# Feeding the projections of a graph layer from an ordered copy of y, made by ScalarE one slot ahead

## What is computed

```python
def _L1_gnn_ref(H, W_lin, W_val, a, W_out, A0, src, dst):
    Xq = (H @ W_lin.T).reshape(bt, n, h, dh)
    Xv = (H @ W_val.T).reshape(bt, n, h, dh)
    e = einsum('behd,hd->beh', leaky_relu(Xq[:, src] + Xq[:, dst], 0.2), a) + log(A0[src, dst] + EPS)
    attn = softmax of e over the edges of one src
    Y = segment_sum(attn[..., None] * Xv[:, dst], src)
    return Y @ W_out.T

x = _layernorm(x + _L0_gnn_ref(x, adj, ...))
x = _layernorm(x + _L1_gnn_ref(x, ...))
```

## Time and profile before

| | us |
|---|---|
| median of three runs | 975.04 (974.39 to 976.59) |
| the profiled execution, time | 973.87 |
| its span, first to last instruction | 972.1 |
| PE busy (matmuls) | 933.5 (96%) |
| PE weight loads | 820.3 (84%) |
| DVE busy | 698.1 (72%) |
| ACT busy | 581.0 (60%) |
| POOL busy | 173.0 (18%) |

### The profile page before, as it was taken

One profiled execution on the slowest core, in us unless ns is written; L12 is line 12 of the kernel. 1 busy time (PEld: TensorE's weight loads), 2 busy tenths in 40 slices (PEclk: granted clock), 3 DMA queues, 4 the chain that ended last, 5 costly groups with the idle time before them and its releaser, 6 DMA issues.

```text
span 972.1 us, 15304 instructions
## 1 busy us (share of the span) xinstructions
PE 933.5 (96%) x5411; PEld 820.3 (84%) x5411; DVE 698.1 (72%) x1560; ACT 581.0 (60%) x1084; POOL 173.0 (18%) x509
## 2 busy tenths in 40 slices
PE   7999999989999999999999999999999999999784
PEld 6888888868777799999988877889989999988674
DVE  5777777777777877777777676675756766765874
ACT  2777777777676766767766666543434445444344
POOL 0000000000000000000000101144434443535655
PEclk9999999999999999999999999999999999999998
DMA  4212211010000000000004776735200101011112
GB/s 114 67 48 65 63 55 45 1 44 1 0 1 1 1 1 1 2 1 1 1 1 87 176 168 154 157 82 130 45 1 12 33 23 33 23 33 34 45 55 66
DMA packets 43260, 45.44 MB, mean 47 GB/s; under 512 B 2576, under 2 KB 40112, under 8 KB 40112
## 3 DMA queue, kind: packets, MB, share of 16 engines
q1 hardware_dynamic: 39504, 27.47, 9.7%
q0 software_dynamic: 2304, 16.78, 8.5%
q10 hardware_dynamic: 1376, 0.22, 0.1%
HBM read 19.29 MB, written 8.39 MB: 28 GB/s over the span
## 4 chain that ended last, share of the span: by engine, by line
PE 86%; DVE 6%; ACT 3%; issue 2%; POOL 2%; DMA 1%; ACTq 0%; DVEq 0%; POOLq 0%
PE psum L1058 12%; PE psum L443 8%; PE psum L444 8%; PE psum L445 8%; PE psum L461 6%; PE psum L457 6%; PE psum L458 6%; PE psum L1131 4%; PE psum L361 3%; PE psum L379 3%; PE psum L389 2%; PE psum L1142 2%; PE psum L352 2%; PE psum L351 2%; PE psum L353 2%
## 5 line engine op out<-in xcount | busy, mean ns | idle before, releaser
L559 ACT ACTIVATE work<-psum,bias 128x512 f32<-128x512 f32 (+1 forms) x408 | 233.7, 623 | 30.7 <-PE psum L461 30.2
L443 PE MATMUL psum<-hT_hi,w_hi 128*128 128x512 f32 (+1 forms) x408 | 148.7, 364 | 3.3 <-ACT work L559 2.6
L444 PE MATMUL psum<-hT_lo,w_hi 128*128 128x512 f32 (+1 forms) x408 | 147.2, 361 | 0.0
L445 PE MATMUL psum<-hT_hi,w_lo 128*128 128x512 f32 (+1 forms) x408 | 147.2, 361 | 0.0
L545 ACT ACTIVATE work<-work 128x512 f32<-128x512 f32 (+1 forms) x112 | 63.8, 570 | 104.5 <-DVE work L811 73.2
L1058 PE MATMUL psum<-w_qv,hT_lo 128*128 128x128 f32 x512 | 124.9, 397 | 1.0 <-DVE hT_lo L1286 1.0
L1058 PEld LDWEIGHTS psum<-w_qv,hT_lo 128*128 128x128 f32 x512 | 122.1, 328 | 1.3 <-DVE hT_lo L1286 1.2
L818 DVE TENSOR_TENSOR work<-work 128x512 f32<-128x512 f32 (+1 forms) x112 | 68.5, 612 | 54.1 <-ACT work L545 54.1
L970 POOL DMA_DIRECT2D hT_lo<-hT_hi x8 | 7.3, 918 | 556.5 <-DVE hT_lo L786 537.3
L457 PE MATMUL psum<-hs_hi,w_hi 128*128 128x512 f32 (+1 forms) x288 | 103.8, 360 | 0.8 <-DVE hs_hi L784 0.6
L461 PE MATMUL psum<-hs_lo,w_hi 128*128 128x512 f32 (+1 forms) x288 | 104.4, 363 | 0.0
(11 more groups left out here) (190 smaller groups left out, 1832.7 us busy)
## 6 DMA issues: line engine op xcount, KB each, us to landing
work<-x SPq DMA_DIRECT2D x32, 256.0 KB, 3.0
x_stage<-x_by_feature SPq DMA_DIRECT2D x8, 1024.0 KB, 5.1
hT_lo<-hT_hi POOLq DMA_DIRECT2D x8, 1024.0 KB, 8.0
hT_lo<-x_stage POOLq DMA_DIRECT2D x8, 1024.0 KB, 7.0
out<-x_kept SPq DMA_DIRECT2D x32, 256.0 KB, 2.3
work<-L_gnn_Wih SPq DMA_DIRECT2D x4, 256.0 KB, 3.2
work<-L_gnn_Whh SPq DMA_DIRECT2D x3, 256.0 KB, 3.0
bg_all<-L_gnn_bg ACTq DMA_DIRECT2D x2, 64.0 KB, 5.1
```

Of the source, the lines that this page charges most:

```text
L443: pe.matmul(out, w_hi[:, w, g, :], xh, start=True, stop=False)
L444: pe.matmul(out, w_hi[:, w, g, :], xl, start=False, stop=False)
L445: mm = pe.matmul(out, w_lo[:, w, g, :], xh, start=False, stop=(t == 0))
L559: op = act.activation(gate[s][g][:, 0:ph.width], psum[:, 4 * s + g, 0:ph.width], ACT.Tanh if g == G else ACT.Sigmoid, bias=bias[:, b:b + 1])
```

## The change

A new tensor `y_ordered` holds two tiles of y with the batch as the slow index and the node as the fast one, so that the columns of a batch are neighbours. ScalarE fills it: `order(k)` is one activation (Copy) of 128 by 512 elements that reads tile k of y four elements apart and writes it in order. It stands at the head of ScalarE's slot k - 1; `order(0)` follows `read_turned(1)` among the last LSTM steps, and `order(1)` opens slot 0. `project` waits for it and takes its stationary operand from the copy, in `queries` and in `values`. The transposes of `turn` go on reading y as before. To make room in SBUF, the ring `x1_kept` has 22 tiles in place of 24.

```diff
-    RING = LAG + 11
+    RING = LAG + 9
+    y_ordered = sb("y_ordered", [P, 2, BT, P])
-    def y_of(k, b):
-        return y_by_feature[:, k * TW:(k + 1) * TW].rearrange("p (t b) -> p b t", b=BT)[:, b, :]
+    def y_of(k):
+        return y_by_feature[:, k * TW:(k + 1) * TW].rearrange("p (t b) -> p b t", b=BT)
...
-                mm = pe.transpose(psum[:, turn_bank(k), b * P:(b + 1) * P], y_of(k, b), ident[:, :])
+                mm = pe.transpose(psum[:, turn_bank(k), b * P:(b + 1) * P], y_of(k)[:, b, :], ident[:, :])
...
         def project(k, bank, w, free, made):
+            pe.wait_ge(S["y_ordered"], k + 1)
             if k:
                 pe.wait_ge(free, k)
             for b in range(BT):
-                mm = pe.matmul(psum[:, bank, b * P:(b + 1) * P], y_of(k, b), w, start=True, stop=True)
+                mm = pe.matmul(psum[:, bank, b * P:(b + 1) * P], y_ordered[:, k % 2, b, :], w, start=True, stop=True)
...
     def enter_read(act, k):
-        read_turned, _ = scalar_steps(act)
+        read_turned, order, _ = scalar_steps(act)
         read_turned(k)
+        if k:
+            order(0)
...
+        def order(k):
+
+            act.wait_ge(S["y_made"], 16 * (k // GROUP + 1))
+            if k >= 2:
+                act.wait_ge(S["v_psum"], k - 1)
+            act.activation(y_ordered[:, k % 2], y_of(k), ACT.Copy).then_inc(S["y_ordered"], 1)
...
         def slot(n):
+            if has(n + 1):
+                order(n + 1)
             if has(n):
```

More of the change, by code:

```diff
@@ L875, in back @@
     last_pass = before.phases[-1]
-    names = ("h_summed x_staged y_made t_psum y_done stats_done q_psum v_psum q_hi xq_ready v_hi xv_ready "
+    names = ("h_summed x_staged y_made y_ordered t_psum y_done stats_done q_psum v_psum q_hi xq_ready v_hi xv_ready "
              "z_psum leaky_ready edges_psum log_added max_f max_b below_max exp_done sum_f sum_b recip_done attn_row attn_psum "
@@ L1248, in slot @@
                 leaky_relu(n, 1)
-        return read_turned, slot
+        return read_turned, order, slot
     def run_scalar(act):
-        _, slot = scalar_steps(act)
+        _, _, slot = scalar_steps(act)
         for n in range(LAST):
```

## The result

| | before | after |
|---|---|---|
| median of the runs, us | 975.18 (974.39 to 976.59) | 921.65 (919.82 to 922.66) |
| the profiled execution, time | 973.87 | 919.82 |
| its span | 972.1 | 918.0 |
| PE busy | 933.5 (96%) | 876.0 (95%) |
| PE weight loads | 820.3 (84%) | 760.3 (83%) |

The ratio is 0.9447 with a 95% interval of 0.9429 to 0.9466: 53.5 us less, where 53.0 had been forecast. The new copy is L1211.

A forecast was written before the change was run, and what follows sets the result against it. PE was taken to bound the kernel through L1058's slow loads; 33.2 + 10.6 + 7.2 + 1.3 + 1.0 - 0.3 = 53.0 us off 973.9 gives 920.9, median 922 us. Own range 913 to 933; 913 to 940 for 8 in 10.

The forecast's parts named there:

- The bound and the cause: Projections in `back`: PE bounds; operand spacing slows L1058, whose matmuls go from 233 to 112 ns, ceiling 62.1 us.
- The rival by which the change does nothing: L1058: spacing is not what slows it, pace stays 233 ns, the copy hides, 975 us; chance 0.07.
- The clock rival: Slots 2 to 12: waits bring the clock down to 1.2 GHz, about 45 us more, 967 us; chance 0.05.
- Full slots: Slots 14 to 31: 1.94 us gained in 16, 1.4 in slots 21 and 29, less 0.6 for late reciprocals: 33.2 us.
- Slots 2 to 7: Early slots: 4.14 us in place of 5.91, with a new 0.16 us PE wait on VectorE; 10.6 us gained.
- Slots 8 to 12: Slots adding softmax steps: VectorE becomes the bound, 24.3 us against 31.5; 7.2 us gained.
- Slots 0 and 1: Start of `back`: one of four halves counts, 1.0 us gained; `order(0)` loses 0.3; `order(1)` costs nothing.
- The copy: ScalarE, ahead of `query_hi` in full slots: 0.7 us, between 0.60 and 1.14, hidden since 1.25 us costs nothing.
- the first rival: Copy dearer than its cover: each us past 1.25 delays `query_hi`, VectorE, PE; at 2 us, 945 us; chance 0.10.
- the slower one: ScalarE stalls reading four apart; slower than before from 3.2 us a copy; at 3.6 us, 988 us; chance 0.05.
- POOL: Early slots: an accumulating DMA may hold it about 1 us; factors asked two slots later, 2 us to spare.
- The ring: Ring of 22: a store has four slots to reuse in place of six; no wait seen, no cost.

The follow-up runs named there:

- run 1: The changed kernel with its copy kept in y's order, so projections still read four elements apart; 974.56 us, ratio 0.9996 to the kernel before.
- run 2: The changed kernel with only `values` reading the ordered copy and `queries` reading y four apart; 948.03 us, ratio 0.9724 to the kernel before.
- Run 11: The changed kernel with the softmax reciprocals done for only 8 of every 128 columns; 920.53 us, ratio 0.9442 to the kernel before.
- run 5: The changed kernel with a cheap copy in y's order, read with neighbouring columns, so projections get other columns; 922.75 us, ratio 0.9474 to the kernel before.
- run 6: The changed kernel with `order(1)` moved to follow `order(0)` among the LSTM gates; 920.81 us, ratio 0.9446 to the kernel before.
- run 12: The kernel before with the ring of 22 tiles and an unused tensor of `y_ordered`'s size; 975.33 us, ratio 1.0006 to the kernel before.
- run 4: The changed kernel with ScalarE also copying one batch (128 elements) beside each copy of tiles 3 to 31; 921.96 us.
- run 3: The changed kernel with ScalarE making each copy of tiles 3 to 31 twice, first into a spare tensor; 925.49 us.
- run 9: On top of run 6, the last four accumulating DMAs spread over slots 1, 4, 8 and 11; 920.73 us, ratio 0.9443 to the kernel before.
- run 7: The changed kernel with `queries(0)`, `values(0)` and `queries(1)` reading y directly, without `order(0)`; 920.14 us, ratio 0.9443 to the kernel before.

## Why the prediction was right

**The bound and the cause** held. The spacing of the stationary operand slowed the loads, and the pace that I took from L1131 is the pace that came. Runs 1 and 2 show it: spacing kept, nothing; half the loads, half the gain. The rival by which the change does nothing is refuted by run 1. The clock rival didn't come either: the mean granted clock is 0.993, with falls of a few us and none through slots 2 to 12. The Trainium skill's "SBUF — State Buffer" (section "Door 1: The DMA port swizzle") can be read so that a step of four fp32 elements is free; run 1 and the changed kernel refute this for weight loads (328 against 194 ns) and for ScalarE (1.14 against 0.63 us). Its other sentence, two accesses to a line, fits both.

**Full slots** were right, and for two small terms too careful. The reciprocal slots pay nothing (7.75; `weight_values` started at 5.01 where 5.15 was reckoned), and slots 21 and 29 gained 1.6 each, not 1.4. That is 0.6 and 0.4, or 1.0 of the 1.1 us between 34.3 and 33.2.

**Slots 2 to 7** were right in size and in kind. `query_lo` ends at s + 3.02 and the first load of `gather` follows at s + 3.07, where 3.02 and 3.08 were reckoned. The slot is 4.12, not 4.14.

**Slots 8 to 12** gave 7.8 for 7.2, but the step was only in part the right one. I took VectorE's total busy time as the bound for all five slots. In fact slots 8 and 9 run at 4.12, and the loss sits in slots 10 to 12. There the chain of waits does lie on VectorE, from 681.8 to 692.2 us, but behind a load of ScalarE's table that the working didn't have. Run 11 took 1.5 us of VectorE's work away and 0.5 came back, as TensorE is close behind. So several things wait on each other in slots 10 to 12, and the near hit owes something to chance.

**Slots 0 and 1** were the step that failed: 0.7 forecast, -0.2 found. That compares one execution with one, and the start of `back` moves by more than this. The stretch from `values(1)` to slot 2 is the better measure: 4.16 us before, 4.51 after, where 1.0 less was forecast. The delay by `order(1)` is free as a wait, as I had said: `values(1)` starts at 639.96, set by VectorE (640.13 before). I left out two things. The first is the same wait of `gather` on `query_lo` that I had reckoned for slots 2 to 7; with it, runs 5 and 6 gain 0.7 of the 1.0. The second is the clock, whose fall cost the other 1.0 in the profiled execution. That the change brings this fall about is not shown. Run 5 had both pauses without it, and run 12, without any copy, had it. Over four executions each, the mean granted clock was 0.992 to 0.994 in the changed kernel and 0.995 to 0.997 in run 6, so it may come more often with `order(1)` in slot 0; but the mean also holds falls elsewhere, such as one in the drain.

**The copy** was mis-sized: 1.14 us, not 0.7. It cost nothing, as runs 4 and 5 show from both sides. The price of a longer one was far too high. I had reckoned that each us past 1.25 is paid in full; run 3 passed it by 1.0 us in 29 slots and paid 3.8 us in all. By this the first rival (2 us, 945 us) and the slower one (deciding at 3.2 us) were priced wrongly: a copy would have to be longer still to undo the gain.

**POOL** was held 2.9 us by a DMA, not 1, and its factors did come late in slot 10, by 0.6 us for VectorE. That the time of slots 10 to 12 didn't suffer is run 9's finding, not the reason I gave (time to spare).

**The ring** and TensorE's extra wait cost nothing, as said (runs 12 and 1). Slot 13 and the drain came out as forecast.

## What to carry to other kernels

When one group of matmuls goes slower than another of the same shape and type, compare their weight loads and the spacing of the stationary operand. If they sit on the path, an ordered copy on an engine with room, made a slot ahead, buys most of the difference (here 53.5 us of the 62.1 on offer). The price of a longer copy is not "everything past the first cover": each engine behind it has slack of its own, and doubling the copy measures it in one run. And where TensorE pauses, its clock can fall in one execution and hold in the next. That moved a stretch of 4 us by 1 us here, so a difference of this size is no finding from one profile of each kernel.

## What the runs showed of the hardware

- A weight load of 128 by 128 fp32 takes 192 to 194 ns with neighbouring columns and 328 ns four elements apart, where each matmul makes two loads; 140 and 206 ns for transposes. Matmuls of 128 columns then follow each other every 112 and 233 ns.
- ScalarE reads 512 fp32 elements a partition, four apart, in 1.14 us, and neighbours in 0.63. VectorE takes 0.62 four apart. No run has VectorE copy neighbours; its casts of the same size (L784) take 0.43, so whether it pays for the spacing is open, and it would be 0.2 us at most by that comparison.
- The granted clock fell to 0.50 for about 3 us after pauses of TensorE of 1.49 and 0.70 us close together, after one of 1.82 (run 7) and after one of 0.91 (run 12). It did not fall after pauses of 1.75 and 1.21 us close together (run 5), nor after one of 1.97 (run 6) or 1.04 (the kernel before). Such a fall cost about 1 us.
- One load of ScalarE's table took 1.28 us. The chain of waits stayed on TensorE at that time before the change, and went through this load after it.
